# Layer 3's edge softmax: stored one-hots, selector products, eight tiles a turn and a scanned maximum

## The chip, the cores and the metric

One core of a Trainium2 chip runs the whole network: TensorE (PE, its weight loads shown as PEld), VectorE (DVE), ScalarE (ACT), GpSimd (POOL), the queue engine SyncE (SP) and 16 DMA engines. The metric is the device time of one execution in microseconds; lower is better.

## The reference, cut to what matters

The network has four graph layers over 6250 nodes of 128 features and 106250 edges; each is followed by a residual addition and preceded by a layer norm with a relu. Layers 0, 1 and 2 are a hypergraph attention with two passes, an edge MLP and a gated edge MLP. Layer 3 is a pair of graph attentions, one for each direction of the edges, with four heads of 32 features:

```python
h = (x @ W).reshape(n, H, C_OUT)
e_src = jnp.sum(h * a_src[None], -1)
e_dst = jnp.sum(h * a_dst[None], -1)
e = leaky_relu(e_src[src] + e_dst[dst], 0.2)
m = segment_max(e, dst)
ex = jnp.exp(e - m[dst])
att = ex / segment_sum(ex, dst)[dst]
out = segment_sum(h[src] * att[:, :, None], dst).reshape(n, H * C_OUT) + b
...
out_fwd = gat(x, W1, ..., src, dst);  out_bwd = gat(x, W2, ..., dst, src)
return 0.5 * out_fwd + 0.5 * out_bwd
```

Every node has a loop edge to itself, so that a segment is never empty.

## The kernel before

**Edges in tiles.** Nodes stand in 49 blocks of 128. The edges are sorted by the block of their receiving node, once by `dst` (order 0) and once by `src` (order 1), and each block's run is padded to a multiple of 256. So there are NT = 928 tiles of 128 edges, two tiles of one block next to each other, and NG = 232 turns of four tiles. The sort writes each record of 16 bytes to DRAM by an indirect DMA of GpSimd (`scatter_po`, L318): 831 for order 0, then 831 for order 1. GpSimd takes the norm's power (`stats_po`) into the second series at t == STATS, 640 of 831.

**Rounds of a sweep.** Each edge pass (a and b for layer 0, twice; c for layer 1; d for layer 2; e for layer 3, twice) is written once per engine as `body(j, u)`. `sweep` emits it for the first turns, then as a hardware loop of U = 8 turns a pass, then for the last ones. `turn(j, u, lag)` gives the turn g = j - lag that a part of the body works on. Engines run their bodies in the order written and meet at semaphores: `S.xt`, `S.tm` and so on count turns, `raised_before(p)` gives their values at the pass's start. Between passes all five engines meet (`meet`). GpSimd's gathers are written out in full, without a loop.

**Pass e, one turn of four tiles.** GpSimd gathers four times 128 rows of 132 numbers by source node (`rows_po`, L408: 128 features, four logits) into a ring of eight turns. VectorE writes the one-hot of the receiving node (L1032), [edge, node] for four tiles. TensorE transposes it into [node, edge] (`turn_pe`, L628) and ScalarE copies it out (L1104). For the maximum ScalarE turns the one-hot into 0 and -1e30 (L1092) and adds the edge's logit, once for each head and tile: sixteen activations of 128 columns (L1099). TensorE transposes the sixteen (L1142), and VectorE takes the maximum over the 256 edges of each block and head from PSUM (L1003, L1021). VectorE then brings the block's running maximum up to date (L1037 to L1054), and computes the old and the new maximum through the leaky relu (L1066 to L1073) and their difference (L1076). TensorE sends the block's receiving logit and new maximum back to the edges by four products of 8 columns (L1131); VectorE forms the exponent (L1009, L1025, L1042, L1057), ScalarE the exponential of 24 columns (L1108: 16 edge weights, 8 factors for the old sums), GpSimd the weighted rows (L987, L989), TensorE their sum by one-hot products (L1123, `eAG`), and VectorE scales the block's old sum and adds (L1017, L1029, L1047, L1062).

**Order of the parts.** The lags are on VectorE 3 for the maximum, 5 for the exponent, 8 for the addition and 0 for the one-hot; on ScalarE 1 for the activations and 5 for the exponential; on TensorE 1, 7, 4 and 2, in this order of the code: transposes of the one-hot, sums, small products, transposes of the logits. The additions and the maximum of one body are interleaved on VectorE by hand.

**Before each e pass** `l3_ve`, `l3_pe`, `l3_ac` and `l3_sp` form h and the logits block by block in thirteen groups, store the table of rows (`HN`) to DRAM, and set the sums in `ACC` to each node's own row (its loop edge).

Of the kernel before, what the change touches and what calls it, by code (L numbers as in the profile page):

```python
# [9 lines left out]
BF16 = mybir.dt.bfloat16  # L10
ALU = mybir.AluOpType
# [16 lines left out]
STATS = 640  # L28
# [9 lines left out]


# [8 lines left out]
    "e": dict(oh=1, pt=1, ot=1, e1=1, e2=1, e3=1, n1=1, xr=1, xt=2, tm=2, m1=1, m2=1, m3=1, m4=1, m5=1,  # L48
              m6=1, ns=1, s2=1, p2=1, ex=1, r=1, ag=1, xa=1, xb=1, xc=1, xd=1),
}  # L50
ORDER = "ababcdee"
RING = {"a": 8, "b": 4, "c": 4, "d": 4, "e": 8}
# [5 lines left out]
def raised_before(p):  # L58

    at = Signals(*(CREDIT + NG * sum(RAISED[k].get(n, 0) for k in ORDER[:p]) for n in NAMES))  # L60
    ring = [sum(64 * len(range(s, NG, RING[k])) for k in ORDER[:p] if s < RING[k]) for s in range(8)]
    return at, ring


def turn(j, u, lag):

    if isinstance(j, int) and not 0 <= j - lag < NG:
        return None
    return j - lag, (u - lag) % U


def sweep(eng, late, body):

    head = -(-(late + 8) // U) * U
    for j in range(head):
        body(j, j % U)
    with eng.Fori(head, NG - U + 1, U) as i:
        for u in range(U):
            body(i + u, u)
    for j in range(NG, NG + late):  # L80
        body(j, j % U)
# [8 lines left out]
def build(nc, a, out):  # L90
# [5 lines left out]
    with ctx:  # L96
        recd = [dram(f"recd{o}", (128 * NT, 4)) for o in range(2)]
        tab = {w: dram(f"tab{w}", (NB * 128, w)) for w in (TW, 128, 256)}
# [17 lines left out]
        nvf = NV[:, :, :].rearrange("p b d -> p (b d)")  # L116
        io4 = iof[:, :].unsqueeze(1).broadcast_to([128, 4, 128])
# [82 lines left out]
        def setup_po(po):  # L200
            for s in S:
                po.drain().then_inc(s, CREDIT)
# [3 lines left out]
                                           base=0, pattern=[[-1, 128]], channel_multiplier=1))  # L206
            own(po, "po", po.memset(LT[:, :], 0.0))
# [178 lines left out]
        def blocks(eng, o, g):  # L386

            _, v = nc.values_load_multi_w_load_instructions(
                BLK[0:1, o, bass.ds(g * 2, 2)], engines=[eng.engine], min_val=0, max_val=NB - 1,
# [13 lines left out]
        def rows_po(po, p, idx, table, G, g):  # L403

            n = RING[ORDER[p]]
            for k in range(4):
# [3 lines left out]
                    in_offset=bass.IndirectOffsetOnAxis(ap=IDX[:, idx, t:t + 1], axis=0)).then_inc(s_ring[g % n], 16)  # L410

# [186 lines left out]
        bEX = room(fb, 4, 4)  # L598
        AGb = lambda r, k: PS[:, 4 + r % 2, 256 * k:256 * k + 129]
# [42 lines left out]
        def b_ve(ve, p):  # L642
            at, ring = raised_before(p)

            def body(j, u):
                if f := turn(j, u, 6):
                    add_ve(ve, at, 1, *f, AGb)
# [31 lines left out]
        def b_ac(ac, p):  # L679
            at, ring = raised_before(p)  # L680

            def body(j, u):
# [5 lines left out]
                if f := turn(j, u, 1):  # L688
                    turned_ac(ac, at, *f, bOT, f[1] % 2)
# [273 lines left out]
        fe = [[WK[:, 0:7900], 0], [hf, 0], [B2[:, 6900:NB * 260], 0]]  # L963
        eG, eOH, eVA, eXR, eOT = room(fe, 8, 4, TW), room(fe, 8, 4, 128), room(fe, NT), room(fe, 2, 16, 128), room(fe, 4, 512)
        eN1, eR = room(fe, 512), room(fe, 2, 4, 133)
        eTM, eE, eLR, eOLD, eT2 = room(fe, 8), room(fe, 16), room(fe, 16), room(fe, 2, 8), room(fe, 2, 8)
        eY, eDD, eEX, eNB = room(fe, 2, 2, 12), room(fe, 8, 24), room(fe, 8, 24), room(fe, 1)
        eSF = B2[:, 0:NB * 8]
        es2 = PS[:, 5, 0:32].rearrange("p (k c) -> p k c", c=8)
        eAG = lambda r, k: PS[:, 6 + r % 2, 256 * k:256 * k + 132]  # L970
        kh = lambda v: v.rearrange("p (k h) -> p k h", h=4)
        ch2 = lambda v: v.rearrange("p k (c h) -> p k c h", h=4)

        def e_po(po, p, o):
            at, ring = raised_before(p)
            meet(po)
            for j in range(NG + 6):
                if j < NG:
                    po.wait_ge(S.r, at.r + j - 7)
# [961 lines left out]
```

## Time and profile before

| | us |
|---|---|
| median of 3 runs | 14173.11 (14166.96 to 14180.73) |
| the profiled execution | 14163.97 |
| its span | 14162.1 |
| PE, DVE, ACT, POOL busy | 8859.2, 9002.0, 5752.0, 9880.4 |
| second scatter of records | from 1194.1 to 2280.8 |
| pass e, first gather, direction 0 and 1 | 10661.8 and 12417.3 |
| pass e, last addition starts | 12351.9 and 14125.1 |

Busy time counts an instruction from start to end on its engine; waits and register work are not in it. "Idle before" is the engine's idle time ahead of an instruction, with what ended it. "Issue" is idle time in which the engine waited for nothing that the profile shows. Several engines overlap, so busy times do not add up to the span. No engine is busy for more than 70% of the whole span; what limits a stretch must be read from that stretch.

### The profile page before, as it was taken

To read this page: it belongs to the slowest core of one execution; us is meant where nothing else is said; L and a number is where in the kernel's file an instruction comes from. 1 tells how busy PE (TensorE), PEld (TensorE's weight loads), DVE (VectorE), ACT (ScalarE), POOL (GpSimd) and SP (SyncE) were. 2 spreads that over 40 slices of the span, in tenths; PEclk is the share of its full clock that TensorE was granted. 3 is DMA by queue.
4 is the path that set the end of the run, shared out by engine and by line. 5 is a ranking of instruction groups with operands and counts; after the bars stand their busy time and mean duration, and the time that the engine had idled before them with its cause. 6 is when DMAs were issued, how large, how long until landed. Compare 5 with 4: busy or idle time off the path is not lost. (4 is left out here: it accounts for less than half of the span.)

```text
span 14162.1 us, 219909 instructions
## 1 busy us (share of the span) xinstructions
PE 8859.2 (63%) x52039; PEld 7904.4 (56%) x52040; DVE 9002.0 (64%) x34342; ACT 5752.0 (41%) x15947; POOL 9880.4 (70%) x10261
## 2 busy tenths in 40 slices
PE   3310003777787567767874666799976777667776
PEld 0000003666676566767773655677756666666666
DVE  9950003777555577765554333699987787777777
ACT  0000002444111144431112222466657888678886
POOL 6777777666677576757774777388856777677775
PEclk9999995777556577766566788899988888888888
DMA  0000001223333422233332223233332111221112
GB/s 16 2 12 2 2 21 35 50 50 48 49 53 52 46 52 51 51 47 52 52 52 36 51 51 50 69 85 84 85 64 55 38 38 39 40 47 38 38 38 39
DMA packets 379414, 629.56 MB, mean 44 GB/s; under 512 B 175970, under 2 KB 243616, under 8 KB 377632
## 3 DMA queue, kind: packets, MB, share of 16 engines
q0 software_dynamic: 305600, 562.74, 21.9%
q1 hardware_dynamic: 73056, 60.09, 1.4%
q14 instruction: 694, 5.69, 0.1%
q8 instruction: 64, 1.05, 0.0%
HBM read 579.16 MB, written 43.08 MB: 44 GB/s over the span
## 5 line engine op out<-in xcount | busy, mean ns | idle before, releaser
L408 POOL DMA_INDIRECT WK<-tab,IDX x6496 | 6423.2, 989 | 2507.9 <-issue 1706.9
L1099 ACT ACTIVATE B<-WK 128x128 f32<-128x128 f32 x7424 | 2219.2, 387 | 479.2 <-PE PS L1142 458.5
L620 PE MATMUL PS<-WK 128*128 128x129 f32 x7424 | 1456.4, 358 | 567.8 <-ACT WK L752 433.6
L620 PEld LDWEIGHTS PS<-WK 128*128 128x128 f32 x7424 | 1296.2, 262 | 718.3 <-ACT WK L752 381.3
L408 POOL DMA_INDIRECT H<-tab,IDX x928 | 930.7, 1003 | 346.3 <-issue 247.9
L1142 PE MATMUL PS<-ident,B 128*128 128x128 f32 x7424 | 1164.6, 324 | 0.0
L1131 PE MATMUL PS<-WK 128*128 128x8 f32 x3712 | 563.9, 279 | 930.7 <-DVE WK L1042 928.8
L1142 PEld LDWEIGHTS PS<-ident,B 128*128 128x128 f32 x7424 | 1093.4, 176 | 0.0
L1131 PEld LDWEIGHTS PS<-WK 128*128 128x128 f32 x3712 | 522.5, 217 | 1020.7 <-DVE WK L1042 965.3
L318 POOL DMA_INDIRECT recd<-B x831 | 847.6, 1020 | 339.5 <-issue 271.3
L704 PEld LDWEIGHTS PS<-B,WK 128*128 128x128 f32 x3712 | 715.4, 288 | 633.8 <-issue 633.6
L704 PE MATMUL PS<-B,WK 128*128 x3712 | 752.1, 324 | 506.4 <-ACT WK L634 504.9
L586 PE MATMUL PS<-WK,B 128*128 128x2 f32 x3712 | 624.1, 290 | 643.3 <-DVE WK L499 642.6
L586 PEld LDWEIGHTS PS<-WK,B 128*128 128x128 f32 x3712 | 613.5, 250 | 738.2 <-issue 412.8
L318 POOL DMA_INDIRECT recd<-REC,B x831 | 803.6, 967 | 276.1 <-issue 276.1
L1003 DVE TENSOR_REDUCE WK<-PS 128x4 f32<-128x1024 f32 x464 | 568.2, 1225 | 603.3 <-PE PS L1142 417.9
L687 ACT ACTIVATE WK<-WK 128x4 f32<-128x4 f32 x464 | 95.3, 205 | 2085.8 <-DVE WK L674 2085.8
L377 ACT ACT_TABLE_LOAD x1 | 1.3, 1283 | 2029.2 <-DVE WK L372 2029.2
L628 PE MATMUL PS<-ident,WK 128*128 128x128 f32 x3712 | 761.8, 343 | 59.8 <-DVE WK L614 58.9
L1211 PE MATMUL PS<-ident,WT 128*128 128x128 f32 x2 | 0.9, 460 | 1254.0 <-ACT H L377 1170.7
L987 POOL TENSOR_TENSOR H<-WK,H 128x512 f32<-128x512 f32 x464 | 489.7, 1055 | 395.0 <-ACT H L1108 389.6
L571 PE MATMUL PS<-B 128*128 128x130 f32 x3712 | 725.8, 361 | 1.4 <-DVE B L502 1.4
(315 smaller groups left out, 22452.2 us busy)
## 6 DMA issues: line engine op xcount, KB each, us to landing
WK<-tab,IDX POOLq DMA_INDIRECT x6496
H<-tab,IDX POOLq DMA_INDIRECT x928
recd<-B POOLq DMA_INDIRECT x831, 2.1
recd<-REC,B POOLq DMA_INDIRECT x831
tab<-B SPq DMA_DIRECT2D x2, 3234.0 KB, 14.4
tab<-WK SPq DMA_DIRECT2D x24, 264.0 KB, 3.3
tab<-WK SPq DMA_DIRECT2D x12, 512.0 KB, 2.9
recd<-REC SPq DMA_DIRECT2D x2, 1856.0 KB, 7.9
```

What stands on the lines that cost most here:

```text
L318: po.indirect_dma_start(out=recd[o], out_offset=bass.IndirectOffsetOnAxis(ap=posi_[o][0:n, t:t + 1], axis=0), in_=rec_[o][0:n, t, :], in_o ...
L408: po.indirect_dma_start(out=G[:, g % n, k, :], out_offset=None, in_=table, in_offset=bass.IndirectOffsetOnAxis(ap=IDX[:, idx, t:t + 1], ax ...
L571: mm = pe.matmul(aAG(r, k // 2), aOH[:, r, k, :], aR[:, r % 2, k, 0:130], start=k % 2 == 0, stop=k % 2 == 1)
L586: mm = pe.matmul(as2[:, k, :], aOT[:, r % 4, 128 * k:128 * k + 128], aY[:, r % 2, k // 2, 1:3], start=True, stop=True)
L620: mm = pe.matmul(AG(r, k // 2), OH[:, r, k, :], R[:, r % 2, k, 0:129], start=k % 2 == 0, stop=k % 2 == 1)
L628: t = pe.transpose(PS[:, bank, 128 * k:128 * k + 128], OH[:, r, k, :], ident[:, :])
L704: mm = pe.matmul(PS[:, 2 + r % 2, k:k + 1], bOT[:, r % 2, 128 * k:128 * k + 128], B2[:, bass.ds(v[k // 2], 1)], start=True, stop=True)
L987: po.tensor_tensor(R4[:, :, :, 0:32], eG[:, r, :, 0:128].rearrange("p k (h c) -> p k h c", c=32), kh(eEX[:, r, 0:16]).unsqueeze(3).broadca ...
L1003: ve.tensor_reduce(eTM[:, 0:4], PS[:, 0:2, :].rearrange("p b (q n) -> p (b q) n", n=256), AX.X, ALU.max).then_inc(S.tm, 1)
L1099: i = ac.activation(eXR[:, r % 2, q, :], eN1[:, 128 * k:128 * k + 128], ACT.Identity, bias=eG[:, r, k, 128 + q % 4:129 + q % 4])
L1131: mm = pe.matmul(es2[:, k, :], eOT[:, r % 4, 128 * k:128 * k + 128], eY[:, r % 2, k // 2, 4:12], start=True, stop=True)
L1142: t = pe.transpose(PS[:, c // 4, 128 * (c % 4):128 * (c % 4) + 128], eXR[:, r % 2, q, :], ident[:, :])
```

## The change

**Turns of eight tiles.** Pass e has NO = 116 turns of eight tiles (four blocks), UO = 4 turns a pass of its loop. `turn` and `sweep` take both numbers as arguments.

**One-hots from DRAM.** Each tile's one-hots are computed once per order and kept in DRAM as bf16 in three forms, per turn of four tiles [128, 3, 512]: turned (node, edge), one minus that, and (edge, node). For order 0 a new sweep (`k_ve`, `k_pe`, `k_ac`, `k_sp`) does it between the sort's rank step and the first norm, while GpSimd scatters order 1's records; order 0's records are loaded first for it, and `STATS` becomes 560. For order 1 it is done inside pass b of layer 0 (`keep`): one more ScalarE copy, two more VectorE operations and one DMA of 393 KB a turn. In pass e SyncE streams two such sets a turn (`e_sp`), in a ring of four.

**Logits spread by products.** A row of the table has 142 numbers: four heads of 32 features and a 1 each, four logits, and the logits again as three bf16 parts (sum equal to fp32). ScalarE copies the 8 x 12 parts out, TensorE transposes them once (96 rows), ScalarE copies that. `spread` then writes in PSUM, for two heads and four tiles, -1e30 times the complement (512 columns) and adds the logit's parts by products with a selector of 96 rows. VectorE's `peak` reduces the PSUM banks as before, 1024 columns, four times a turn.

**Maximum by a scan.** `eMX` holds for every group and head nine numbers: what comes in, and for each of four blocks its receiving start value and the block's peak. One `tensor_tensor_scan` of 36 numbers with `eB9` (0, or -1e30 where a block begins) takes the running maximum over the turn.

**The rest.** The receiving logit and the new maximum go back to the edges in three bf16 parts each, by 16 products of 12 columns. The weighted rows are formed by ScalarE: 32 activations of 33 columns with the weight as scale, which also write the weight itself (the 1). GpSimd only gathers. `l3_*` builds the parts, run boundaries, selector and per-block rows by some 40 more small operations and 9 products.

```diff
+        TB = [B2[:, 100 + 768 * i:868 + 768 * i].bitcast(BF16).rearrange("p (s c) -> p s c", s=3) for i in range(4)]
...
+        def k_ve(ve):
+            def body(j, u):
+                if f := turn(j, u, 0):
+                    g, r = f
+                    kept(ve, 0, g, r)
+                    ve.tensor_tensor(TB[r % 4][:, 2, :].rearrange("p (k n) -> p k n", n=128), io4, low(0, g),
+                                     ALU.is_equal).then_inc(s_kh, 1)
+                if f := turn(j, u, 2):
+                    g, r = f
+                    ve.wait_ge(s_kt, CREDIT + g + 1)
+                    ve.tensor_scalar(TB[r % 4][:, 1, :], TB[r % 4][:, 0, :], -1.0, 1.0, ALU.mult,
+                                     ALU.add).then_inc(s_kn, 1)
...
         def e_ve(ve, p, o):
             at, ring = raised_before(p)
 
+            def peak(g, s):
+
+                b, i = 2 * (s % 2), s // 2
+                ve.wait_ge(S.xt, at.xt + 4 * g + s + 1)
...
+            def add(v, g, r, i):
+
+                d = accf[:, bass.ds(v[i] * 133, 132)]
+                d4 = d.rearrange("p (h c) -> p h c", c=33)
+                f4 = eEX[:, r, 32 + 4 * i:36 + 4 * i].unsqueeze(2).broadcast_to([128, 4, 33])
+                ve.wait_ge(S.xb, at.xb + 4 * g + i)
+                ve.tensor_tensor(d4, d4, f4, ALU.mult).then_inc(S.xc, 1)
+                ve.wait_ge(S.xc, at.xc + 4 * g + i + 1)
+                ve.tensor_tensor(d, d, eAG(i), ALU.add).then_inc(S.xb, 1)
+
             def body(j, u):
-                m, e, x, f = turn(j, u, 3), turn(j, u, 5), turn(j, u, 8), turn(j, u, 0)
-
+                m, e, x = turn(j, u, 1, NO, UO), turn(j, u, 2, NO, UO), turn(j, u, 4, NO, UO)
...
+                    peak(gm, 0)
+                if x:
+                    gx, rx = x
+                    vx = blocks(ve, o, gx, 4)
+                    ve.wait_ge(S.ag, at.ag + gx + 1)
+                    add(vx, gx, rx, 0)
+                    add(vx, gx, rx, 1)
+                if m:
+                    peak(gm, 1)
...
+                if x:
+                    add(vx, gx, rx, 3)
                 if e:
                     ve.wait_ge(S.e3, at.e3 + ge + 1)
...
+                    ve.tensor_tensor(eE, eLR, eS2[:, :, 1, :], ALU.subtract).then_inc(S.p3, 1)
                 if m:
+                    peak(gm, 2)
+                if e:
+                    ve.wait_ge(S.p3, at.p3 + ge + 1)
+                    ve.tensor_scalar(eDD[:, re_, 0:32].rearrange("p (k h) -> p k h", h=4), eE, 0.0, None,
+                                     ALU.min).then_inc(S.p2, 1)
+                if m:
+                    peak(gm, 3)
...
+                    ve.tensor_tensor_scan(sc, eB9[:, run(g36, 36)], sc, 0.0, ALU.add, ALU.max).then_inc(S.m1, 1)
...
+        def e_ac(ac, p, o, d):
             at, ring = raised_before(p)
 
             def body(j, u):
...
+                e, t = turn(j, u, 2, NO, UO), turn(j, u, 0, NO, UO)
+                for k in range(8):
+                    if e:
...
+                        if k % 4 == 0:
+                            ac.activation(eOHF[:, q, k:k + 4, :].rearrange("p k n -> p (k n)"), eSTb[:, r, k // 4, 2, :],
+                                          ACT.Copy)
+                        if k == 0:
+                            ac.wait_ge(S.m5, at.m5 + g + 1)
+                            ac.wait_ge(S.p2, at.p2 + g + 1)
+                            ac.activation(eEX[:, r, :], eDD[:, r, :], ACT.Exp).then_inc(S.ex, 1)
+                            ac.wait_ge(S.ex, at.ex + g + 1)
+                        for h in range(4):
+                            i = ac.activation(eR[:, q, k, 33 * h:33 * h + 33], eG[:, r, k, 33 * h:33 * h + 33], ACT.Copy,
+                                              scale=eEX[:, r, 4 * k + h:4 * k + h + 1])
...
+                    if t and k == 1:
...
+                        ac.activation(eES.rearrange("p (k c) -> p k c", c=12), eGb[:, rt, :, 272:284], ACT.Copy).then_inc(S.oh, 1)
+                    if t and k == 4:
+                        ac.wait_ge(S.pt, at.pt + gt + 1)
+                        ac.wait_ge(S.xt, at.xt + 4 * gt - 4)
+                        ac.activation(eET[0:96, rt % 2, :], PS[0:96, 4, 0:64].bitcast(BF16), ACT.Copy).then_inc(S.ot, 1)
...
+            def spread(g, r, s):
+
+                b, i = 2 * (s % 2), s // 2
+                pe.wait_ge(S.tm, at.tm + 4 * g + s - 1)
+                for h in range(2):
+                    pe.matmul(PS[:, b + h, :], eNBI, eSTb[:, r, i, 1, :], start=True, stop=False)
+                    for k in range(4):
+                        c = 4 * (4 * i + k) + b + h
+                        mm = pe.matmul(PS[:, b + h, 128 * k:128 * k + 128], eSEL[0:96, c:c + 1].broadcast_to([96, 128]), eET[0:96, r % 2, :],
+                                       start=False, stop=k == 3)
+                mm.then_inc(S.xt, 1)
+
             def body(j, u):
...
```

TensorE's new body j is, in this order: the 16 small products of turn j-2 (waits `S.ns`), spread(j-1, 2), spread(j-1, 3), the sums of turn j-3 (waits `S.r`), the transpose of turn j's parts (waits `S.oh`), spread(j, 0) and spread(j, 1) (wait `S.ot`).

## Rows read from the trace of the kernel before

**Rows 1.** windows: length, PE, PEld, DVE, ACT, POOL busy us, clock, DMA share, GB/s

```profile
1300.00:1600.00 300.00, 0.00 (x0) 0.00 (x0) 0.00 (x0) 0.00 (x0) 223.94 (x233) 1.00 0.03 2
...
4000.00:4500.00 500.00, 397.90 (x1940) 364.56 (x1940) 278.94 (x1066) 73.16 (x193) 382.06 (x388) 0.60 0.33 52
...
10700.00:12320.00 1620.00, 1166.31 (x8102) 1108.55 (x8102) 1290.37 (x4951) 1355.35 (x4287) 1213.61 (x1352) 0.85 0.20 38
```

**Rows 2.** two lines of layer 3, by direction: ns min/median/max, first and last start

```profile
L408 POOL DMA_INDIRECT WK<-tab,IDX x928: 940/953/1457, 10661.8 to 12313.9; - x186
...
L1062 DVE TENSOR_TENSOR ACC<-ACC,PS x232: 281/285/292, 10715.8 to 12351.9; 128x132 f32 x116
...
L408 POOL DMA_INDIRECT WK<-tab,IDX x928: 940/952/1470, 12417.3 to 14088.3; - x186
...
L1062 DVE TENSOR_TENSOR ACC<-ACC,PS x232: 280/285/293, 12470.6 to 14125.1; 128x132 f32 x116
```

**Rows 3.** timeline, one turn of layer 3: start us, us, instructions, idle before

```profile
11500.00 4.78 ACT L1099 ACTIVATE B<-WK 128x128 f32<-128x128 f32 x16
...
11503.40 0.16 DVE L1042 TENSOR_TENSOR WK<-WK,PS 128x16 f32<-128x16 f32 x1
...
11503.61 1.06 PE L1131 MATMUL PS<-WK 128*128 128x8 f32 x8 [2.39 <-DVE WK L1042]
...
11506.06 1.23 DVE L1003 TENSOR_REDUCE WK<-PS 128x4 f32<-128x1024 f32 x1 [0.62 <-PE PS L1142]
...
11506.75 1.07 PE L1123 MATMUL PS<-H 128*128 128x132 f32 x8
...
11509.98 0.16 DVE L1042 TENSOR_TENSOR WK<-WK,PS 128x16 f32<-128x16 f32 x1
```

**Rows 4.** waits, 11000 to 12000 us: who waited for whom, us, times, longest

```profile
DVE WK L1003 <- issue: 56.1, 15, 4.1
```

**Rows 5.** timeline behind the end of a pass of the loop

```profile
11519.44 1.88 PE L1131 MATMUL PS<-WK 128*128 128x8 f32 x8 [5.04 <-DVE WK L1042]
```

**Rows 6.** instructions by shape, 11000 to 12000 us: count, busy us, mean ns, idle before

```profile
L1099 ACT ACTIVATE B<-WK 128x128 f32<-128x128 f32 x2208 | 660.0, 387 | 149.8 <-PE PS L1142 147.1
...
L1003 DVE TENSOR_REDUCE WK<-PS 128x4 f32<-128x1024 f32 x139 | 170.2, 1225 | 177.3 <-PE PS L1142 121.1 <-issue 56.1
...
L1092 ACT ACTIVATE WK<-H,WK 128x512 f32<-128x512 f32 x139 | 99.0, 712 | 0.1
...
L1108 ACT ACTIVATE H<-H 128x24 f32<-128x24 f32 x139 | 29.3, 211 | 19.3 <-DVE H L1057 19.3
```

**Rows 7.** timeline at the end of layer 3's first direction

```profile
12348.89 0.30 DVE L1017 TENSOR_TENSOR ACC<-ACC,H 128x132 f32 x1 [0.46 <-DVE ACC L1062]
12349.22 0.29 DVE L1029 TENSOR_TENSOR ACC<-ACC,PS 128x132 f32 x1
12349.66 0.29 DVE L1047 TENSOR_TENSOR ACC<-ACC,H 128x132 f32 x1
...
12350.82 0.30 DVE L1017 TENSOR_TENSOR ACC<-ACC,H 128x132 f32 x1 [0.55 <-PE PS L1123]
```

**Rows 8.** instructions by shape, 0 to 1200 us, bf16 products and weight loads

```profile
L300 PE MATMUL PS<-H,WK 128*128 128x490 bf16 x50 | 29.0, 589 | 0.0
...
L300 PEld LDWEIGHTS PS<-H,WK 128*128 128x128 bf16 x50 | 5.2, 104 | 23.8 <-DVE H L251 23.8
```

**Rows 9.** VectorE's waits, 9500 to 10000 us (layer 2)

```profile
DVE ACC L607 <- issue: 22.9, 81, 0.7
```

**Rows 10.** timeline, start of layer 3's preparation

```profile
10620.56 5.49 DVE L1703 MEMSET ACC<- 128x6517 f32 x1 [1.31 <-issue]
```

**Rows 11.** DMA issues: line, count, KB each, median us to landing

```profile
xs<-X SPq DMA_DIRECT2D x1, 3136.0 KB, 10.8
```

**Rows 12.** the page, costliest groups: the two scatters

```profile
L318 POOL DMA_INDIRECT recd<-B x831 | 847.6, 1020 | 339.5 <-issue 271.3
...
L318 POOL DMA_INDIRECT recd<-REC,B x831 | 803.6, 967 | 276.1 <-issue 276.1
```

More of the change, by code:

```diff
@@ L58, in raised_before, with turn, sweep @@
 def raised_before(p):
[L60 to L61 removed]
+    at = Signals(*(CREDIT + sum(TURNS[k] * RAISED[k].get(n, 0) for k in ORDER[:p]) for n in NAMES))
+    ring = [sum((128 if k == "e" else 64) * len(range(s, TURNS[k], RING[k])) for k in ORDER[:p] if s < RING[k])
+            for s in range(8)]
     return at, ring
[L65 to L74 removed]
+def turn(j, u, lag, n=NG, unroll=U):
+    if isinstance(j, int) and not 0 <= j - lag < n:
+        return None
+    return j - lag, (u - lag) % unroll
+def sweep(eng, late, body, n=NG, unroll=U):
+    head = -(-(late + unroll) // unroll) * unroll
     for j in range(head):
[L76 to L78 removed]
+        body(j, j % unroll)
+    with eng.Fori(head, n - unroll + 1, unroll) as i:
+        for u in range(unroll):
             body(i + u, u)
[L80 to L81 removed]
+    for j in range(n, n + late):
+        body(j, j % unroll)
 def staged(t, lag):
@@ new lines, in k_ac, with body, k_sp @@
+        def k_ac(ac):
+            def body(j, u):
+                if f := turn(j, u, 0):
+                    g, r = f
+                    ac.wait_ge(s_kp, CREDIT + g + 1)
+                    ac.activation(TB[r % 4][:, 0, :], PS[:, r % 2, 0:256].bitcast(BF16), ACT.Copy).then_inc(s_kt, 1)
+            sweep(ac, 0, body)
+        def k_sp(sp, o):
+            for g in range(NG):
+                sp.wait_ge(s_kn, CREDIT + NG * o + g + 1)
+                sp.dma_start(oht[o][g], (bTB if o else TB)[g % 4]).then_inc(s_kd[g % 4], 16)
@@ L415, in build, with k_done @@
+        def k_done(sp, o):
+            for i in range(4):
+                sp.wait_ge(s_kd[i], 16 * (NG // 4) * (o + 1))
         fa = [[WK[:, 0:7900], 0], [B2[:, 200:NB * 260], 0]]
@@ L974, in e_po, with run, streamed, came @@
+        def run(start, n):
+            return slice(start, start + n) if isinstance(start, int) else bass.ds(start, n)
+        def streamed(eng, d, g, r):
+            base = 16 * NGR + 16 * (NO // 4) * d
+            eng.wait_ge(s_st[r], base + 16 * (g // 4 + 1) if isinstance(g, int) else (g - r) * 4 + (base + 16))
+        def came(eng, g, r, ring):
+            eng.wait_ge(s_ring[r], ring[r] + 128 * (g // 4 + 1) if isinstance(g, int) else (g - r) * 32 + (ring[r] + 128))
         def e_po(po, p, o):
@@ L1145, in e_pe @@
+                    pe.wait_ge(S.ot, at.ot + g)
+                    pe.transpose(PS[0:96, 4, 0:64].bitcast(BF16), eES, identb).then_inc(S.pt, 1)
+                if f := turn(j, u, 0, NO, UO):
+                    g, r = f
+                    streamed(pe, d, g, r)
+                    pe.wait_ge(S.ot, at.ot + g + 1)
+                    spread(g, r, 0)
+                    spread(g, r, 1)
             meet(pe)
-            sweep(pe, 7, body)
+            sweep(pe, 3, body, NO, UO)
         def turn4(pe, bank, T, n):
```

437 lines of the change are left out of this document (261 added, 176 removed).

## The prediction

> **What bounds the kernel now.** I read the stages first [rows 1]. While the second scatter runs, GpSimd issues 233 indirect DMAs in 300 us and nothing else runs: 1.29 us each. In order 1 of layer 0 (4000 to 4500 us) it issues 388 in 500 us, again 1.29 each, with VectorE at 279 us and ScalarE at 73. Both stretches hang on GpSimd's issue rate. Layer 3 is another matter: from 10700 to 12320 us every engine has time left (TensorE 1166 us of 1620, VectorE 1290, ScalarE 1355, GpSimd 1214), so a ring of waits sets the pace. Its two edge loops go from the first gather to the last addition, 10661.8 to 12352.2 and 12417.3 to 14125.4 [rows 2]: 1690 and 1708 us, mean 1699, or 7.3 us for each of 232 turns of four tiles.
>
> In an undisturbed turn [rows 3] VectorE subtracts the maximum (L1042) at 11503.40, TensorE starts its small products (L1131) behind that and then the transposes, VectorE reduces (L1003) at 11506.06 and is at L1042 again at 11509.98. The ring is 6.58 us. The mean is longer because VectorE idles before L1003 for no reason that the profile shows, 15 times in 1000 us, at most 4.1 us [rows 4]: once per pass of its loop of eight turns. After such a gap TensorE needs 1.88 us for a group that took 1.06 [rows 3, 5]. So eight tiles cost 2 x 6.58 = 13.2 us and about 1.4 on top.
>
> **The new turn of eight tiles, as a ring.** What decides is the order in which each engine meets its parts of the turns, so I follow body j on all three. VectorE's body j starts with the first peak of turn j-1, which waits for TensorE's spread(j-1, 0). Later in the same body comes the minimum of turn j-2 (p2). ScalarE's body j waits for just this p2 before its exponential, and only behind 20 of its 32 scaled copies and two other copies does it copy the turned logits of turn j (ot). TensorE's spread(j, 0) waits for that, and VectorE's body j+1 for the spread. Nothing of it overlaps from one turn to the next; the pieces add up.
>
> VectorE, peak to p2. A reduction of 1024 PSUM columns takes 1.225 us [rows 6], three of them lie here: 3.5, as the next may start a little before the end. Four blocks are multiplied and added, each two dependent instructions of 132 columns. The end of the old loop shows these alone [rows 7]: 0.33 us from multiplication to addition, 0.44 from there to the next block's multiplication, so 0.77 a block, 3.1. Loading two block numbers costs what is left from 12349.66 + 0.33 + 0.29 to 12350.82, 0.54, and less where it lies behind a reduction; for four I take 0.4. The 192-column reduction: 1.225 less 832 columns at 1.04 ns, 0.36. Four small operations mostly overlap others. Sum 7.4; bounds 7.0 (load hidden) and 8.2 (no overlap).
>
> ScalarE, p2 to ot. A copy of 128 columns with one operand from a pointer takes 387 ns [rows 6], and sixteen come in 4.78 us [rows 3], 299 each. 512 columns take 712 [rows 6]: 0.85 ns a column. So 33 columns come every 299 - 95 x 0.85 = 218 ns; twenty, 4.4. Exponential 0.21 to 0.23 [rows 6] and the wait for itself: 0.3. The 96-column copy 0.2, the second unpacking of 512 columns 0.54, the 128-column copy from PSUM 0.28. Sum 5.7; bounds 5.4 and 6.1.
>
> TensorE, ot to peak: for each of two heads one product of 512 bf16 columns and four of 128. The trace has bf16 products of 490 columns, 589 ns for one with its filling, and bf16 weight loads of 128 columns in 104 [rows 8], which is the pace of 1.2 GHz. At that level 2 x (0.43 + 4 x 0.107) + 0.2 = 1.9, at 2.4 GHz 1.05. Which one? At the upper level TensorE has four spreads of 0.95, sixteen small products (1.0) and eight fp32 ones of 132 columns (2 x 1.07 [rows 3]): 6.9 us in a ring of 15, and its idle time lies in one piece of some 5 us before spread(j, 0), broken by one short transpose. The old gap of 5.04 us left it slow [rows 5]. I take 1.75, the lower level most of the time.
>
> With 0.2 for the hand-overs the ring is 7.4 + 5.7 + 1.75 + 0.2 = 15.1 us. Beside it stand GpSimd's 8 gathers, 10.3; VectorE's whole body, 7.4 + the fourth peak 1.2 + nine dependent steps of 0.2, 10.4; ScalarE's 32 x 0.218 + 2.3 = 9.3. All fit inside. GpSimd's old multiplication (L987) goes, worth nothing where GpSimd waits anyway.
>
> The gap at a pass's end: VectorE has it in layer 3 (22 instructions a turn, eight turns a pass) and not in layer 2, where the longest unexplained wait is 0.7 [rows 9] (20 a turn, eight turns). The new pass has 26 a turn and four turns, fewer than either. Rows leave it at 0 to 4 us per four turns; I take 0, and VectorE's 4.6 us of slack would hide one. The Trainium skill ("Runtime: NRT & Kernel Launch", "Instruction fetch mechanics") says that a taken branch stalls when its target is no longer among the two held pages of 256 instructions; by it the shorter pass has no gap, and by the row alone it might.
>
> The loop: first gather to first spread 8 x 1.25 + 4.6 = 15 us, turn 1 some 10 later, 114 rings, less 5 for the first without additions, 28 until the last turn has run out. 48 + 114 x 15.1 = 1769 us against 1699: **+70 each, +140 for both.**
>
> **Layer 3's preparation.** It starts with a memset of 5.49 us [rows 10], covered by weight loads. In its place come VectorE's constants (26 tiny dependent steps of 0.2 in the first direction) and the run boundaries (eight operations of 464 columns of about 0.65 and a memset of the bf16 table, 2 to 4): the weights' product waits for them, 6 us later in the first direction, 2 in the second. Behind the last group four dependent splits stand before the table's store, 2.5, and the store is 8% wider, 1. The eight fp32 products of 464 columns and their copies (15 to 18) run beside the store of some 14. **+18 for both**; bounds +5 and +60.
>
> **Building the stored one-hots.** Order 0's are built beside the second scatter: per turn a comparison, four transposes, a ScalarE copy, a negation and a store of 393 KB. 3136 KB took 10.8 us [rows 11], so 1.4 at that rate and 3 with latency, four in flight: 1.9 us a turn, 440 and some loop ends. The statistics' product now stands behind 560 scatters of (803.6 + 276.1) / 831 = 1.30 us [rows 12], 728 us, so GpSimd will not wait. What it can cost is GpSimd's rate: the first scatter, with VectorE busy, has 1020 ns each, the second, with it idle, 967 [rows 12]. 53 ns on 370 scatters at three fifths of that activity: +12; bounds 0 and +67 (232 negations of 0.29, fully lost). Order 1's are built inside layer 0's loop: VectorE 2.9 + 1.2 us of 5.15 a turn, ScalarE 0.75 + 0.6, 76 GB/s of stores. GpSimd needs a turn's rows back after 15 us and has them after about 6, so again only its rate suffers: +12; bounds 0 and +140.
>
> The Trainium skill ("SBUF — State Buffer", "Who interferes with whom") says that VectorE in a two-port mode, which copies and one-source operations can enter, holds GpSimd off for the whole instruction and starves its descriptors. By it both stretches would grow by nearly the locked time, some 200 us in all, which is rival D. The row, whose busy time includes such casts, says 53 ns a DMA.
>
> **Sum.** 140 + 18 + 24 = +182 on the profiled execution of 14163.97 us (span 14162.1): 14346. The median before, 14173.11, is 9 above it: 14355, rounded to 14350.
>
> **Rivals.**
> A, the other side: the ring closes in less than the old pace. With 42 us for the rest, break-even is 48 + 114 r = 1699 - 21, r = 14.3. The place is TensorE's level before spread(j, 0) and the block load on VectorE: at 2.4 GHz (0.7 less) and with the load hidden (0.4 less) r is 14.0, with ScalarE at its lower bound 13.7; at 13.9 the loops take 1633 each and the total is 14173 - 132 + 42 = 14083. For it: gaps of 2.4 us mostly leave TensorE at full pace. Against: this gap is twice that. 0.26, of which 0.06 within 28 us of before.
> B: the bodies do not chain as I read them and the busiest engine sets the pace, about 11 us: 48 + 114 x 11 = 1302, total 14173 - 794 + 42 = 13421. Only a misreading of the order allows it. 0.05.
> C: more is late than the ring: TensorE stays at 1.2 GHz throughout (13.7 us of work, its small products end after VectorE wants them), or stalls at its own loop's end, 4 us in every four turns of which 3.5 show. r = 16.2, the loops 1895, total 14173 + 392 + 42 = 14607. For it: TensorE's ring part has no slack behind spread(j, 1). 0.18.
> D: GpSimd is starved in the two builds, or the stores outlast the 728 us: up to +200, total 14550. 0.06.
>
> **How the numbers follow.** The forecast is r from 14.5 to 15.8, total 14220 to 14510, with 0.45. For 8 in 10 the range takes in A's 14083 and C up to its middle: 14060 to 14620. Faster or slower by over 0.2% (28 us) is about what a measurement can tell. Faster, A's larger part and B: 0.25. The same, A's edge: 0.06. Slower, the forecast, C and D: 0.69.
>
> **What would show it.** In a middle turn of the changed kernel: ScalarE's exponential right behind VectorE's minimum, its copy of the turned logits 5.7 us later, TensorE's 512-column product behind that, and VectorE's first peak waiting for it with 4 to 5 us idle; the spacing of that peak is r. GpSimd at about 70% in the loop, waiting for ScalarE. No gap of 4 us at the pass's end. DMAs in the two builds every 1.30 to 1.35 us. It is wrong if VectorE has next to no idle time before the first peak (B), if spread(j, 0) takes 1 us everywhere (A), if the ring opens by 3 us at every fourth turn (C), or if the time ahead of layer 3 grows by over 60 us (D).

## The result and the profile after

The changed kernel takes 14310.01 us (median of 4 runs, 14303.44 to 14313.4) against 14172.4 for the kernel before: ratio 1.0096, 95% interval [1.0079, 1.0114]. It is slower by 138 us, about 1%. Forecast were 14350 (14060 to 14620) and slower at 0.69. The profiled execution has a span of 14301.5 us, 139.4 more than before. First a stretch of layer 3's first direction and one of the second scatter (windows), then the gathers and additions of the first loop (ns min/median/max, first and last start):

```profile
10800.00:12380.00 1580.00, 971.10 (x7793) 704.63 (x7792) 978.82 (x2773) 905.65 (x3926) 812.91 (x854) 0.77 0.35 93
1300.00:1600.00 300.00, 97.72 (x644) 55.36 (x644) 157.79 (x424) 96.52 (x162) 227.78 (x218) 1.00 0.58 218
...
L1095 POOL DMA_INDIRECT B<-tab,IDX x928: 942/945/1072, 10707.1 to 12393.0; - x186
...
L1126 DVE TENSOR_TENSOR ACC<-ACC,PS x464: 291/293/296, 10758.7 to 12446.5; 128x132 f32 x155
```

Every engine works less than before [rows 1] (VectorE 979 us of 1580, ScalarE 906, GpSimd 813), and yet the loop is longer: 10707.1 to 12446.8 is 1739.7 us, against 1690 in [rows 2]. A ring still sets the pace. One turn of it, on VectorE (L1113 the first peak, L1164 the minimum), ScalarE (L1216 the exponential, L1231 the turned logits) and TensorE (L1243, the 512-column product), which answers to [rows 3]:

```profile
11601.61 1.23 DVE L1113 TENSOR_REDUCE WK<-PS 128x1024 f32 x1 [4.50 <-PE PS L1246]
...
11608.50 0.17 DVE L1164 TENSOR_SCALAR B<-B 128x32 f32<-128x32 f32 x1
...
11608.70 0.24 ACT L1216 ACTIVATE B<-B 128x48 f32<-128x48 f32 x1 [6.31 <-DVE B L1164]
...
11613.94 0.26 ACT L1231 ACTIVATE H<-PS 96x128 bf16<-96x128 bf16 x1
11614.18 0.94 POOL L1095 DMA_INDIRECT B<-tab,IDX  x1 [0.30 <-issue]
11614.44 0.50 PE L1243 MATMUL PS<-H,B 128*128 128x512 bf16 x1 [3.17 <-ACT H L1231]
...
11616.39 1.23 DVE L1113 TENSOR_REDUCE WK<-PS 128x1024 f32 x1 [4.50 <-PE PS L1246]
```

From peak to peak it is 14.78 us, in three pieces: 7.06 on VectorE (first peak to the end of the minimum), 5.53 on ScalarE (to the end of the turned logits), 2.19 on TensorE (to the next first peak), each hand-over counted in the piece behind it. Over 103 turns of this direction they average 7.09, 5.53 and 2.23, together 14.85. The waits of 1000 us (11200 to 12200; total, times, longest) show that each of the 67 turns in it has this shape:

```profile
ACT B L1216 <- DVE B L1164: 421.6, 67, 6.5
...
POOL B L1095 <- ACT B L1219: 341.1, 67, 5.4
...
DVE WK L1113 <- PE PS L1246: 303.5, 67, 4.6
...
DVE WK L1113 <- issue: 3.7, 1, 3.7
...
PE PS L1243 <- ACT H L1231: 211.1, 67, 3.2
```

Where the 139 us come in, read from GpSimd's work by stretch:

| stretch | before | after | difference |
|---|---|---|---|
| start to the first gather of layer 0 | 2286 | 2279.1 | -7 |
| from there to the last norm's start | 8305.7 | 8343.1 | +37 |
| layer 3's two preparations | 61.9 + 65.1 | 76.8 + 79.9 | +30 |
| its two loops | 1690 + 1708 | 1739.7 + 1737.9 | +79 |

### The profile page after: what moved, and what is told of

Its sections match the earlier page's. It is cut to its first block and busy times, and to the rows that moved or that the text cites. A ratio compares the mean times of both kernels' runs of the same rounds, so it can differ in the third digit from the quotient of the medians.

```text
span 14301.5 us, 217644 instructions
## 1 busy us (share of the span) xinstructions
PE 8748.2 (61%) x53251; PEld 7258.3 (51%) x53252; DVE 8835.8 (62%) x31209; ACT 5195.7 (36%) x16189; POOL 9157.5 (64%) x9335
## 5 line engine op out<-in xcount | busy, mean ns | idle before, releaser
L419 POOL DMA_INDIRECT WK<-tab,IDX x4640 | 4520.4, 974 | 1902.6 <-issue 1304.4
L1095 POOL DMA_INDIRECT B<-tab,IDX x1856 | 1769.3, 953 | 1812.3 <-ACT B L1219 1102.2
L1113 DVE TENSOR_REDUCE WK<-PS 128x1024 f32 (+1 forms) x928 | 1132.2, 1221 | 1079.0 <-PE PS L1246 1075.3
L692 PEld LDWEIGHTS PS<-WK 128*128 128x128 f32 x7424 | 1305.6, 263 | 733.0 <-ACT WK L834 380.5
L1219 ACT ACTIVATE B<-B 128x33 f32<-128x33 f32 x7424 | 1671.0, 309 | 7.5
L1243 PE MATMUL PS<-H,B 128*128 128x512 bf16 x1856 | 1010.5, 544 | 891.9 <-ACT H L1231 681.4
L1246 PEld LDWEIGHTS PS<-H,B 96*128 96x128 bf16 x7424 | 808.6, 130 | 418.1 <-issue 349.0
L1246 PE MATMUL PS<-H,B 96*128 96x128 bf16 x7424 | 1013.0, 280 | 0.0
L1243 PEld LDWEIGHTS PS<-H,B 128*128 128x128 bf16 x1856 | 229.3, 124 | 966.6 <-issue 749.1
L641 PEld LDWEIGHTS PS<-B 128*128 128x128 f32 x3712 | 687.0, 275 | 2.3 <-DVE B L572 2.3
L612 ACT ACTIVATE WK<-WK 128x128 f32<-128x128 f32 x1856 | 593.0, 390 | 205.9 <-DMA WK<-tab,IDX 178.1
## 6 DMA issues: line engine op xcount, KB each, us to landing
tab<-B SPq DMA_DIRECT2D x2, 3479.0 KB, 21.5
```

Source lines behind the costliest of these rows:

```text
L419: po.indirect_dma_start(out=G[:, g % n, k, :], out_offset=None, in_=table, in_offset=bass.IndirectOffsetOnAxis(ap=IDX[:, idx, t:t + 1], ax ...
L641: mm = pe.matmul(aAG(r, k // 2), aOH[:, r, k, :], aR[:, r % 2, k, 0:130], start=k % 2 == 0, stop=k % 2 == 1)
L692: mm = pe.matmul(AG(r, k // 2), OH[:, r, k, :], R[:, r % 2, k, 0:129], start=k % 2 == 0, stop=k % 2 == 1)
L1095: po.indirect_dma_start(out=eG[:, g % 4, k, :], out_offset=None, in_=tab[TW3], in_offset=bass.IndirectOffsetOnAxis(ap=IDX[:, o, t:t + 1], ...
L1113: ve.tensor_reduce(eM2[:, g, b:b + 2, 2 * i:2 * i + 2, 1] if isinstance(g, int) else eM2[:, bass.ds(g, 1), b:b + 2, 2 * i:2 * i + 2, 1].re ...
L1219: i = ac.activation(eR[:, q, k, 33 * h:33 * h + 33], eG[:, r, k, 33 * h:33 * h + 33], ACT.Copy, scale=eEX[:, r, 4 * k + h:4 * k + h + 1])
```

## The experiments

They ran on four chips. On two of them (e1 to e6) every kernel is longer, the one before too (16356 and 16093 us); on the other two (e7 to e12) it takes 14164 and 14169, as in the first measurement. So each number stands beside the kernel before on its own chip, and the order of telling starts with the chips that are like the first. On e1 to e4's chip the changed kernel itself was not run.

**e8 and e7: the level.** e8 is the changed kernel with a small GpSimd instruction behind every second gather:

```diff
+                        if k % 2 == 1:
+                            own(po, "po", po.memset(B2[:, 9836:9837], 0.0))
```

> The changed kernel with a GpSimd memset of one word, waited for, behind every second gather of layer 3; GpSimd has 4.6 us to spare in a turn. Theory of a hold by unbroken runs of gathers: the wait of 3.9 us in front of VectorE's small-products reduction goes, a turn takes 14.9 us instead of 18.7, and both loops together 2 x 114 x 3.8 = 870 us less than e5: ratio to the kernel before about 1.025. Rival (the hold has nothing to do with the gathers being unbroken): a turn stays at 18.7 or grows by the memsets, ratio 1.08 or more.

> The kernel before, unchanged, for its profile where the experiments run. In e5 one wait of 3.9 us stands in every turn of the new loop in front of VectorE's reduction of the small products (18.67 us a turn against 14.85), and it ends 1.4 to 1.8 us behind the last of the turn's eight gathers. Theory of a hold: something of TensorE's results is kept back while GpSimd issues indirect DMAs without a break; the old layer-3 loop has a GpSimd multiplication behind every four gathers, so it should be spared: loops of about 1700 us or less, while layer 0 (no GpSimd work between gathers) is as slow as in e5, pass a about 1670 us. Rival (TensorE's clock or this place as such): the old loops are longer too, by 2 us a turn of four tiles or more, 2100 us each.

e8: 14305.84 us, ratio 1.0107 [1.009, 1.0124], 14.88 us a turn (mean of 104); the changed kernel in its first measurement has 14.85. e7 (one run): 14159.52, its loops 1690 and 1713 us from the first gather to the last addition, against 1690 and 1708 in [rows 2]. The chip showed nothing of what the two were to test, so the theory of a hold is not tested by them. They give the level for e9 and e10, and they show that GpSimd has time left: four memsets a turn cost nothing that the total shows.

**e10: the turned logits later.** The ring theory says that every copy ahead of the turned logits is paid in full.

```diff
-                    if t and k == 4:
+                    if t and k == 7:
                         ac.wait_ge(S.pt, at.pt + gt + 1)
```

> e1's order (turned logits behind all 32 copies) with e8's memsets. In e1 the 2.6 us did not show (19.2 us a turn against e5's 18.7), which the hold explains by a second, longer ring over the gathers that has 2 us of cover for it. With the hold gone the ring theory asks for 14.9 + 2.6 = 17.5 us a turn against e8's 14.9; the rival (an engine's own work sets the pace) for e8's turn.

Measured: 14880.13 us (one run), 574 above e8, and 17.44 us a turn (mean of 98) against 14.88. ScalarE's exponential (L1218 in both) and turned logits (L1233), e10 first, then e8:

```profile
11505.35 0.24 ACT L1218 ACTIVATE B<-B 128x48 f32<-128x48 f32 x1 [8.80 <-DVE B L1166]
11513.15 0.25 ACT L1233 ACTIVATE H<-PS 96x128 bf16<-96x128 bf16 x1
11522.91 0.24 ACT L1218 ACTIVATE B<-B 128x48 f32<-128x48 f32 x1 [9.00 <-DVE B L1166]
```

```profile
11514.29 0.24 ACT L1218 ACTIVATE B<-B 128x48 f32<-128x48 f32 x1 [6.21 <-DVE B L1166]
11519.53 0.25 ACT L1233 ACTIVATE H<-PS 96x128 bf16<-96x128 bf16 x1
11529.32 0.24 ACT L1218 ACTIVATE B<-B 128x48 f32<-128x48 f32 x1 [6.46 <-DVE B L1166]
```

Exponential to turned logits grew from 5.24 to 7.80, by 2.56, and so did the turn, though ScalarE does the same work and then waits 2.6 us longer. An engine's own work can't be what sets the pace: the ring's forecast of 17.5 came, the rival's unchanged turn did not.

**e9, e11 and e12: the ring cut open.** ScalarE's body begins with the next turn's two copies, ahead of its wait for the minimum, and TensorE transposes ahead of its sums:

```diff
                 e, t = turn(j, u, 2, NO, UO), turn(j, u, 0, NO, UO)
+                if t:
+                    ...
+                    ac.activation(eES.rearrange("p (k c) -> p k c", c=12), eGb[:, rt, :, 272:284], ACT.Copy).then_inc(S.oh, 1)
+                    ac.wait_ge(S.pt, at.pt + gt + 1)
+                    ac.wait_ge(S.xt, at.xt + 4 * gt - 4)
+                    ac.activation(eET[0:96, rt % 2, :], PS[0:96, 4, 0:64].bitcast(BF16), ACT.Copy).then_inc(S.ot, 1)
                 for k in range(8):
```

e9 has e8's memsets too, e12 only those behind the fourth and the eighth gather, e11 none.

> e4's order (turned logits first) together with e8's memsets. Ring and hold theories both right: the turn is the largest of the engines' own work, now GpSimd with 8 gathers at 1.25 and 4 memsets at about 0.3, 11.2 us, or VectorE's 9.1 to 10.4: 2 x 114 x 7.5 = 1700 us less than e5, ratio to the kernel before 0.97 (0.965 to 0.99). If the memsets don't end the hold: 1.03, as e4. If the ring was not what held the turn: as e8.

> e4's kernel once more, without memsets. If the chip is like that of e7 to e10: e9's turn is 10.78 us, VectorE's own chain of a turn without waits 10.35 (first peak to first peak), and GpSimd's pair of gathers with memset 2.6 to 2.7, so both are close to setting it. Without the memsets GpSimd needs 10.0 and VectorE alone is left: 10.4 a turn, 2 x 114 x 0.4 = 90 us less than e9, 13320, ratio to the kernel before 0.940. If GpSimd's memsets cost nothing: 0.947. If the chip is like that of e4 to e6: 1.03 again.

> The same with a memset behind the fourth and the eighth gather only. On a chip like that of e7 to e10: between e9 and e11, 10.5 us a turn, ratio 0.943. On a chip like that of e4 to e6 this is the test of the hold: if a memset or a short pause of GpSimd releases what waits, four gathers (5 us) are the longest hold instead of eight, a turn falls from 15 us to 11 to 12.5 and the ratio to 0.96 to 0.99; if it does not, 1.03 as e11.

Measured: e9 13410.01 us, ratio 0.9467 [0.9451, 0.9482]; e11 13406.73, 0.946 [0.9444, 0.9476]; e12 13415.26, 0.9466 [0.945, 0.9481]. The turn is 10.78, 10.74 and 10.82 us. e9 is 896 us below e8 on the same chip; the forecast of e4 for this order had been 870. e9's own forecast, 0.97 (0.965 to 0.99), was made for the chips of e4 to e6 and missed: the time lies below it. All three beat both kernels by over 5%. e11's forecast of 90 us less without memsets was wrong, and so was e12's of 10.5 us and 0.943: the three times agree within their intervals. e11's other branch, 0.947 if the memsets cost nothing, came. e9's windows and, of its timeline, two first peaks:

```profile
11000.00:11800.00 800.00, 599.87 (x5349) 490.28 (x5462) 690.21 (x1942) 646.60 (x2764) 599.95 (x897) 0.82 0.46 128
```

```profile
11401.53 1.23 DVE L1115 TENSOR_REDUCE WK<-PS 128x1024 f32 x1
...
11411.88 1.23 DVE L1115 TENSOR_REDUCE WK<-PS 128x1024 f32 x1
```

VectorE is busy for 690 us of 800, no bracket of idle time stands at either of these two peaks, and 10.35 us lie between them: its own body, which the prediction had put at 10.4. The mean turn is 10.78, because in other turns VectorE still waits for a spread:

```profile
DVE WK L1115 <- PE PS L1247: 16.9, 29, 1.2
```

That is 16.9 us in the 74 turns of these 800 us, about half of the 0.43 us by which the mean turn exceeds 10.35; the rest was not taken apart.

**e5 and e6: the other chips.** The changed kernel and e4's order (that of e11) on the second of the two chips with longer times.

> The changed kernel once more, with nothing edited. Where the first four experiments ran, the kernel before took 16356 us instead of 14173: the layers ahead of the edit took longer as well (pass a of layer 0: 1709 us of gathers instead of 1254), so their totals can't be set against 14310. If that belongs to the place and not to the kernels, and this run meets it again, the ratio to the kernel before shows what the change does there: by the ring theory e1 less 2 x 114 x 2.6 = 17200 us, ratio 1.05. If the run meets the conditions of the first measurement, 14310 and 1.010 come back.

> e4's kernel beside the changed kernel in the same conditions. Ring theory: the turn falls from 14.85 us to the largest of the engines' own work, 10.4 to 11 us; loops 48 + 114 x 11 = 1302 against 1739: 870 us less than e5 (between -750 and -1100), 13440 where e5 has 14310. Turns of 9.1 us occurred in e4, so VectorE's and GpSimd's own work may allow less than 10.4: then about -1100. Rival (a pause or a transfer holds every turn at 14.8): within 100 us of e5.

e5: 17375.39 us, ratio 1.0798 [1.078, 1.0816]; e6: 16588.45, 1.0311 [1.0294, 1.0328]. There the change costs 8%, not 1%, which neither branch of e5's text had (1.05 and 1.010). e6 is 787 us below e5, inside its 750 to 1100, but both ends of that step lie elsewhere than forecast: 18.7 us a turn in e5 and 14.9 in e6, where single turns take 9 to 22.5. e5's turn is 18.70 us (mean of 102), 3.9 more than 14.85, and that is one wait per turn (13400 to 14400 us):

```profile
DVE B L1146 <- remote: 205.4, 53, 4.5
```

"Remote" is a release that belongs to no recorded instruction. L1146 reduces the small products, whose own records end about 6 us earlier. In time it stands behind GpSimd's last gather of the turn (e5's timeline):

```profile
13901.07 0.94 POOL L1095 DMA_INDIRECT B<-tab,IDX  x1 [0.30 <-issue]
...
13903.42 0.36 DVE L1146 TENSOR_REDUCE B<-PS 128x64 f32<-128x192 f32 x1 [3.74 <-remote]
...
13906.64 0.24 ACT L1216 ACTIVATE B<-B 128x48 f32<-128x48 f32 x1 [10.06 <-DVE B L1164]
...
13919.61 0.95 POOL L1095 DMA_INDIRECT B<-tab,IDX  x1 [0.30 <-issue]
...
13922.00 0.36 DVE L1146 TENSOR_REDUCE B<-PS 128x64 f32<-128x192 f32 x1 [4.34 <-remote]
```

It resumes 1.4 us behind the end of the last gather in both turns, and within 1.4 to 1.6 us of it in most turns of e5. So in e5 a second ring closes there: exponential to first gather 4.2, eight gathers 9.7, 1.4, reduction to the next exponential 3.2, together 18.5. The one-hot builds show late results too, without any gather table or loop of layer 3. Windows of e5, with the scatter running and with the scatter at rest (behind its 560th DMA GpSimd waits for the norm's statistics, from 1997 to 2375 us), and then the same builds of the changed kernel in its first measurement:

```profile
1800.00:1900.00 100.00, 5.34 (x36) 3.12 (x36) 8.25 (x18) 5.37 (x9) 73.15 (x72) 1.00 0.11 37
2100.00:2200.00 100.00, 35.82 (x237) 20.29 (x236) 52.94 (x119) 35.23 (x59) 0.00 (x0) 1.00 0.57 232
```

```profile
1200.00:1300.00 100.00, 35.82 (x236) 20.30 (x236) 52.47 (x119) 34.84 (x59) 77.67 (x74) 1.00 0.62 230
```

Nine turns per 100 us while GpSimd scatters, 59 once it rests; on the first chip 59 beside the scatter. The granted clock is 1.00 in all three. One round of e5's builds shows whose result is late: TensorE's four transposes and ScalarE's copy of them, which had been waiting:

```profile
1818.43 0.58 PE L460 MATMUL PS<-WT,B 128*128 128x128 bf16 x4 [10.68 <-issue]
...
1828.89 0.60 ACT L470 ACTIVATE B<-PS 128x512 bf16<-128x512 bf16 x1 [10.61 <-issue]
```

That is 9.9 us between result and use, while the other hand-overs of the round take under 0.2. So on these two chips some of TensorE's results reach the other engines late while GpSimd issues indirect DMAs. The end of GpSimd's run is not what frees them in general. In the scatter the waits end every 11 us while the DMAs go on, and in e2 (below, the same chip as e1) 96 of 160 such waits in front of L1146 end while further gathers of the same run follow, as here:

```profile
14021.11 0.95 POOL L1095 DMA_INDIRECT B<-tab,IDX  x1 [0.30 <-issue]
14021.35 0.36 DVE L1146 TENSOR_REDUCE B<-PS 128x64 f32<-128x192 f32 x1 [2.41 <-remote]
...
14022.36 0.94 POOL L1095 DMA_INDIRECT B<-tab,IDX  x1 [0.30 <-issue]
```

What the cause is, and whether a pause of GpSimd ends the wait, stays open: e8, e9, e10 and e12 carried the pause, and ran where nothing was late. Nor was the kernel before profiled on such a chip, so the 8% can't be divided between the loops and the builds, beside which GpSimd rests for some 375 us.

**e1 to e4: one piece moved at a time**, on the first of these chips, and so read against e5's 1.0798 and 18.70 us, from the other one. How far that carries is seen in the one kernel that ran on both: 15.6 us a turn in e4, 14.9 in e6. e1 is e10's edit, e4 is e11's kernel. e2 moves both copies forward, e3 the minimum:

```diff
-                    if t and k == 1:
+                    if t and k == 0:
...
-                    if t and k == 4:
+                    if t and k == 1:
```

```diff
-                if m:
-                    peak(gm, 2)
                 if e:
                     ve.wait_ge(S.p3, at.p3 + ge + 1)
                     ...
+                if m:
+                    peak(gm, 2)
```

> ScalarE's copy of the turned logits stands behind all 32 scaled copies of the turn instead of behind 20; nothing else changes. Theory (the ring peak -> minimum -> exponential and copies -> turned logits -> spread -> peak sets the pace): 12 copies at 0.22 us lengthen the ring by 2.6 us, from 14.8 to 17.4 a turn, 114 turns and two loops: +600 us, 14910. Rival (an engine's own work or the gathers set the pace): ScalarE has as many instructions as before, so no change, 14310 within 30.

> The same copy stands behind 8 scaled copies instead of 20, and the copy that feeds the transpose behind 4 instead of 8. Theory: 12 copies at 0.22 us and the second unpacking of 512 columns, 0.54, leave the ring: 14.8 - 3.2 = 11.6 us a turn, which is still above GpSimd's 8 gathers (10.3): 2 x 114 x 3.2 = -730 us, 13580 (13500 to 13750, if the gathers or the transpose come late). Rival (an engine's own work sets the pace): no change, 14310.

> VectorE takes the minimum of the edge logits before its third peak reduction of the turn instead of behind it. Theory: one reduction of 1.22 us leaves the ring: 14.8 - 1.2 = 13.6 a turn, -280 us, 14030. If the ring went through TensorE and ScalarE alone, or an engine's own work set the pace, no change: 14310.

> The two copies for the next spread stand at the head of ScalarE's body, before its wait for the minimum, and TensorE's transpose before its sums. Theory: the ring is cut open: spread(j, 0) then waits for VectorE's third peak only, and what is left is each engine's own work: VectorE 9.2 us busy of a turn plus its waits for itself, about 10.4; GpSimd's 8 gathers 10.3. About 11 us a turn, 48 + 114 x 11 = 1302 for a loop that takes 1739 now: 14310 - 870 = 13440 (13300 to 13700). Rival (contention or the streamed loads hold the turn at 14.8): within 100 of 14310.

| | ratio to before [95%] | us a turn | forecast | argued from e5's second ring |
|---|---|---|---|---|
| e1 | 1.0884 [1.0866, 1.0902] | 19.4 | +2.6 | its first ring is 17.5, below 18.6 |
| e2 | 1.0598 [1.0581, 1.0616] | 17.6 | -3.2 | unchanged |
| e3 | 1.0678 [1.066, 1.0695] | 18.07 | -1.2 | -1.2, and 0.5 given back |
| e4 | 1.0339 [1.0322, 1.0356] | 15.6 | -3.8 | partly open |

The last column is not shown. In e1 the second ring of e5 does not close at all: in 1000 us L1146 waits 8 times and 4.9 us in all, and the late results stand in front of the peaks instead. In e2 and e4 part of the waits stand before other readers of TensorE's results. The signs in the ratios are those forecast, the sizes are not, and e1's +0.7 and e3's -0.6 us are no larger than the difference between e4 and e6: none of these four can be used for the price of a piece. e1 and e10 differ only in e10's memsets; the 2.6 us show in e10, where nothing is late. Turns of e4 vary between 9 and 23 us.

## Why the prediction was right

**The sum.** Forecast +182, measured +139: the two loops 61 less, layer 3's preparation 12 more, everything before it 6 more (+30 for +24). The 61 are the ring, whose turn came out 0.25 us shorter, in 2 x 114 turns, 57 us. The 6 are partly luck, see the builds.

**The ring (step right, sizes within 0.35 us).** Forecast 7.4 + 5.7 + 1.75 + 0.2 = 15.1, measured 14.85 over 104 turns. The waits show one chain through all three engines, e10 shows that ScalarE's piece adds to it in full, and e9 and e11 that with the chain cut the turn falls to VectorE's own work. No run on a chip like the first moved VectorE's piece alone (e3 ran where results were late). VectorE's piece was 7.06 for 7.4: the minimum starts 0.08 before the third peak ends, and the block load stood behind a reduction, costing 0.2 of the assumed 0.4. ScalarE's 5.5 for 5.7: the copies of 33 columns come every 0.22 us, as worked out. TensorE's 2.19 for 1.95 went the other way. Its 512-column products started 0.73 to 0.85 us apart from 11614.44 on, against 0.45 in the middle of the same turn. That is the pace of the lower clock level, and the granted clock (in windows the third column from the end: 0.50 is the lower level, 1.2 GHz, and 1.00 the upper, 2.4) says the same. In the turn shown it fell as the spread began, but in most turns it fell in the idle stretch ahead of it: in 83 of 108 turns before the spread's first product, by up to 2.9 us. Four windows of such a turn, whose spread begins at 11019.83: with TensorE's one transpose, idle, with the two spreads, and with what follows them:

```profile
11015.30:11017.20 1.90, 0.26 (x1) 0.12 (x1) 1.44 (x9) 1.90 (x11) 0.00 (x0) 1.00 0.00 0
11017.40:11019.70 2.30, 0.00 (x0) 0.00 (x0) 0.00 (x0) 2.30 (x12) 1.08 (x2) 0.50 0.00 0
11019.80:11023.90 4.10, 4.07 (x37) 2.87 (x38) 1.78 (x3) 2.86 (x12) 3.19 (x4) 0.50 0.42 74
11024.10:11030.50 6.40, 3.95 (x36) 3.04 (x34) 5.98 (x15) 1.47 (x7) 3.12 (x4) 1.00 0.47 164
```

It came back while TensorE was at work, 3 us or more behind the spread's start. That was the point on which rival A hung, and it decided against it: with A's 1.05 the turn would have been 13.9 and the total, as an estimate, 14310 - 2 x 114 x 0.94 = 14096, faster than before. VectorE's idle 4.5 us before the first peak is what was named as the sign; GpSimd's 70% was not, it is busy for 51%, as only 0.94 of a gather's 1.25 us counts.

**The loop.** 48 + 114 x 14.85 = 1741 against 1739.7 and 1737.9 measured. +70 each was forecast; it is +50 and +30: each is 28 us shorter by the ring's 0.25 us, and the forecast was set against the mean of two directions of which the second was already 18 us longer.

**The gap at the pass's end.** Taken as 0, and none is left, where [rows 4] has fifteen in 1000 us: the one wait of 3.7 us without a visible end is the usual wait for a turn's first peak, the 68th beside the 67 listed. The DMA queue of instructions says why (before, then after, 11200 to 12200 us: packets, MB, share):

```profile
q14 instruction: 94, 0.77, 0.3%
```

```profile
q14 instruction: 5, 0.04, 0.0%
```

Each of the sixteen gaps of the old loop in this stretch has two or three of the 94 packets in it: it fetched instructions anew in every pass, and the new one does not. By the rule of the Trainium skill ("Runtime: NRT & Kernel Launch", "Instruction fetch mechanics") a taken branch stalls when its target page is no longer held; the packets agree. The reason in the prediction, VectorE's instruction count, was argued and not shown.

**Layer 3's preparation (the term that was too small).** +18 forecast, +30 measured, 15 for each direction. The single terms given add up to 15 only (9.5 and 5.5); where the other 3 come from the prediction does not say. In the first direction the group loop and its forerunners took 7.5 us more, where 8.5 was said, and in the second 7.9, where 4.5 was said; the store of the table did the rest. Issue and landing, before and after:

```profile
tab<-B SPq DMA_DIRECT2D x1, 3234.0 KB, 14.1
```

```profile
tab<-B SPq DMA_DIRECT2D x1, 3479.0 KB, 21.4
```

8% more bytes took 52% longer, where +1 us was forecast. Two things differ: the rows have 568 bytes instead of 528, and the eight new products with their copies run beside the store, where TensorE and ScalarE did nothing before. The rate stays low when those are through, which speaks for the rows. Windows before and after, with all engines at rest:

```profile
10656.00:10658.00 2.00, 0.00 (x0) 0.00 (x0) 0.00 (x0) 0.00 (x0) 0.00 (x0) 0.50 1.24 276
```

```profile
10702.00:10704.00 2.00, 0.00 (x0) 0.00 (x0) 0.00 (x0) 0.00 (x0) 0.00 (x0) 0.50 0.98 130
```

No run tried another row length, so this stays argued.

**The builds.** +24 forecast. The second scatter took 1108.2 us instead of 1086.7, +21.5 (forecast 12): 218 DMAs in the 300 us in which [rows 1] has 233. Order 1's, which stand in the first pass b, cost +11.0 there, forecast 12; the second pass b, where nothing was added, changed by -5.9. From e7 to e8 the same two differences are +4.0 and -2.6, so a few us of either belong to the execution. The first scatter came out 29 us shorter with unchanged code (again from e7 to e8); that stays unexplained, and it is what made the start 7 us shorter. The one-hots took 1.72 us a turn, 400 us, far inside the 728. The Trainium skill ("SBUF — State Buffer", "Who interferes with whom") says that VectorE in a two-port mode holds GpSimd off for a whole instruction; the estimate from it was some 200 us for both builds, rival D. The runs show 21.5 and at most 11 us, about a sixth of that, and do not tell whether this is the port or the stores. Another +32 stand in the layers beside them (18 in the first pass a, 12 in the second, 4 between the first pass b and the second pass a), in code whose text the diff leaves alone; from e7 to e8 the two passes a differ by 18 and 10 again, and no experiment took them apart. The -29 and the +32 had no term in the forecast and nearly cancel: that the time ahead of layer 3 came within 6 us is luck.

**The rivals.** B's 11 us is the pace of e9 and e11, once the order of the bodies is changed; with the order as written it was out. C and D did not come on the first chip. On the second chip with longer times (e5) something like C did, a wait of 3.9 us in nearly every turn, but for results whose products had ended 6 us before, and with it the time lies outside the range. So the forecast holds for chips like the first; nothing in it allowed for the others.

## What to carry to other kernels

Halving the number of turns pays only if the chain that runs through a turn is cut as well: write down, for each engine, what stands between the thing that it waits for and the thing that the next engine waits for, and move everything else behind. Here two copies of 0.27 us at the wrong place of ScalarE's body, with the transpose between them on TensorE, cost 4 us a turn, 900 us in all. When an ordering is to be judged, test it in both directions: the lengthened ring (e10) is evidence of the cause as much as the shortened one. And run the unchanged kernel on the same chip as the variants: without it, e1 to e4 gave no price for anything.

## What the runs showed of the hardware

- On two of four chips some results of TensorE reached other engines late while GpSimd issued indirect DMAs: 6 us behind the last product in e5's loop (a wait of 3.9 us a turn), 9.9 us in its scatter. In e5's loop the wait ended 1.4 to 1.6 us behind the last gather, in e2's mostly with more gathers of the same run to come. The same kernel had ratio 1.0096 on one chip and 1.0798 on another.
- TensorE's granted clock was at the lower level during the first spread of nearly every turn of the changed kernel. It fell between 2.9 us before and 1.1 us behind the spread's start; the stretch ahead of the spread holds nothing of TensorE but one transpose. It came back with TensorE at work, 3 us or more behind the spread's start (108 turns, 10800 to 12400 us).
- A store with rows of 568 bytes ran at 163 GB/s, one with rows of 528 at 229 (3479 KB in 21.4 us, 3234 KB in 14.1).
- In 1000 us of the old layer-3 loop, 94 instruction packets and sixteen gaps of up to 3.9 us on VectorE, with two or three packets in each gap; in the new loop 5 packets and no such gap.
- A GpSimd memset of one word behind a gather took 0.11 us and moved the next gather back by 0.08 (1.33 us from gather to gather instead of 1.25).
